# Expert buffers with two experts' rows side by side in 944 slots, and the first expert layer on 64-row tiles

## The chip, the cores and the metric

One NeuronCore of one Trainium2 chip runs the whole program in one launch. The metric is device time in microseconds (us) of that core. The kernel before took 1568.96 us, the median of 3 runs (1568.46 to 1574.54).

## What is computed

Two layers over x with batch B = 8, length L = 750, width D = 64, float32: a dilated convolution, attention and a switch feed-forward (layer 0), then phase attention and a second mixture of experts (layer 1), each added to the running activations `h`. The change is in the layer-0 feed-forward, which sends each of the 6000 tokens to one of 8 experts, with a capacity of C = 938 tokens for each:

```python
C = max(1, math.ceil(1.25 * T / E))                      # T = 6000, E = 8: 938
idx = jnp.argmax(probs, axis=-1)                         # expert of each token
pos = (jnp.cumsum(one_hot, axis=0) * one_hot).sum(-1).astype(jnp.int32) - 1
kept = pos < C
buf = jnp.zeros((E, C, D), dtype=h.dtype).at[idx, pos_safe].set(x, mode='drop')
hmid = jax.nn.relu(jnp.einsum('ecd,edf->ecf', buf, w1) + b1[:, None, :])   # F = 256
ybuf = jnp.einsum('ecf,efd->ecd', hmid, w2) + b2[:, None, :]
y_tok = ybuf[idx, jnp.minimum(pos, C - 1)] * (prb * kept)[:, None]
```

## The kernel before

The instructions of each engine are written out in order, with semaphores between them. Activations `H` and normalized ones `XN` lie in on-chip memory as 125 partitions x 6 tiles for each batch. Two buffers lie in DRAM: `xbuf` (the page calls it expert_in) and `ybuf` (expert_out), each of 8 experts x 1000 rows of 64 floats.

**The start.** GpSimd clears the conv matrix, the identity and a 125 x 512 block `zeros`. SP's queue then issues, in this order: the convolution's small loads, eight fills of `xbuf` with zeros (L972), 18 preparation loads (`prep`, L976: Q, K, VO and small weights), and the later weights (`wd`, L978). TensorE runs nine dependent convolution steps (L517); after step 4's matmuls it waits for all `prep` loads and transposes Q and K (L528), and goes on with step 5. The attention's small copies of row maxima (L988) come behind all of these on SP.

**Routing.** Beside the attention of batch b + 1, and for the last batch behind all attention, VectorE finds each token's expert. GpSimd adds up the one-hot rows of the tiles (kind "choose"), TensorE turns them into positions, GpSimd computes `slot_in` and `slot_out` (kind "slots", ten small operations, each linked to the one before), and issues six scatters of 125 rows into `xbuf` (L1182).

**The expert stage.** After the last attention step GpSimd clears `w1p`; SP waits for that and loads the expert weights: `w1p` holds for each expert a 128-row matrix with its 64 rows in the half that its data use and zeros in the other, `w2e` the second layer. When all 48 scatters have landed, SP loads `xbuf` into `XB` (L1002): expert e in columns 0 to 63, e + 4 in columns 64 to 127, row c x 125 + r of an expert in partition r, chunk c; eight loads. TensorE waits for all eight, transposes 8 chunks for each of four pairs into `XBT` (L737), and waits for the weights. Then it goes on in the order in(0), in(1), out(0), in(2), out(1), back(0), in(3), out(2), back(1), out(3), back(2), back(3). `expert_in` (L748) is 8 matmuls over 128 rows and 469 columns, `expert_out` (L760) 8 matmuls, two in column halves of a bank, `expert_back` (L772) 8 transposes. A float32 matmul is two instructions in the profile. ScalarE and VectorE empty the eight PSUM banks in turn. SP stores a pair as two transfers (L1009) when both its `yb` banks are emptied. GpSimd waits for all eight stores and gathers token rows (L1202), on which the second layer of the network stands.

```python
sp.dma_start(xbuf[e * ROWS:(e + 1) * ROWS].rearrange("(r c) d -> r (c d)", r=R), zeros)          # L972
pe.wait_ge(S["xb_loaded"], 16 * 8)
pool.wait_ge(S["y_stored"], 16 * 8)
```

Of the kernel before, what the change touches and what calls it, by code (L numbers as in the profile page):

```python
# [17 lines left out]
ALU = mybir.AluOpType  # L18
ACT = mybir.ActivationFunctionType
# [11 lines left out]
CAP = -(-(5 * B * L) // (4 * E0))  # L31
CH = CAP // 2
ROWS = 1000
PH, PP, WN = 4, 32, 5
# [16 lines left out]
def build(nc, t, out):  # L51
    with ExitStack() as ctx:
# [115 lines left out]

        w1p, at = view(0, [E0, F0])
        w2e, at = view(at, [E0, 2, D])  # L170
        XB, at = view(at, [4, 8, 128], parts=R)
        XBT, at = view(at, [4, ROWS])
        HM, at = view(at, [2, 2, 2, CAP])
        YT, at = view(at, [4, ROWS])
# [51 lines left out]
        def sem(*names):  # L226
# [12 lines left out]
            "att_h", "rc_ready", "lnb_sum", "lnb_x", "lnb_ssq", "lnb_done", "onehot_sum", "pos_ready", "memory", "big_set", "dma_prep")  # L239
        sem("late_zero", "w_late", "big", "route_ld", "route_ex", "onehot", "slots", "scattered", "xb_loaded",  # L240
            "y_stored", "gathered0", "gathered1", "gathered2", "gathered3",
# [263 lines left out]
        def _(pe):  # L505
# [225 lines left out]

            pe.wait_ge(S["xb_loaded"], 16 * 8)
            for e in range(4):
                for h in range(2):
                    ps, done = take(pe, ("xbt", e, h))
                    for n in range(4):
                        last = pe.transpose(ps[:, n * R:(n + 1) * R], XB[:, e, 4 * h + n, :], ident[0:R, 0:R])  # L737
                    last.then_inc(done, 1)
            pe.wait_ge(S["w_late"], 16 * 3)

            def expert_in(e):
                emptied(pe, ("xbt", e, 0))
                emptied(pe, ("xbt", e, 1))
                for a in range(2):
                    for fh in range(2):
                        for nn in range(2):
                            ps, done = take(pe, ("h1", e, a, fh, nn))
                            pe.matmul(ps[:, 0:CH], w1p[:, e + 4 * a, fh * 128:(fh + 1) * 128],  # L748
                                      XBT[:, e, nn * CH:(nn + 1) * CH], start=True, stop=True).then_inc(done, 1)

# [14 lines left out]
            def expert_back(e):  # L765
                emptied(pe, ("y", e, 0))
                emptied(pe, ("y", e, 1))
                pe.wait_ge(S["big"], 2)
                for h in range(2):
                    ps, done = take(pe, ("yb", e, h))  # L770
                    for n in range(4):
                        last = pe.transpose(ps[0:R, n * 128:(n + 1) * 128],  # L772
                                            YT[:, e, (4 * h + n) * R:(4 * h + n + 1) * R], ident)
                    last.then_inc(done, 1)
# [183 lines left out]
        def _(sp):  # L958
# [12 lines left out]
            for e in range(E0):  # L971
                sp.dma_start(xbuf[e * ROWS:(e + 1) * ROWS].rearrange("(r c) d -> r (c d)", r=R), zeros)\  # L972
                    .then_inc(S["xbuf_zero"], 16)
# [18 lines left out]

            sp.wait_ge(S["late_zero"], 1)
            sp.dma_start(w1p[0:64, 0:4, :], t["L0_ffn_w1"][0:4].rearrange("e d f -> d e f")).then_inc(S["w_late"], 16)
            sp.dma_start(w1p[64:128, 4:8, :], t["L0_ffn_w1"][4:8].rearrange("e d f -> d e f")).then_inc(S["w_late"], 16)
            sp.dma_start(w2e.rearrange("f e h d -> f (e h) d"),
                         t["L0_ffn_w2"].rearrange("e (h f) d -> f (e h) d", h=2)).then_inc(S["w_late"], 16)
            sp.wait_ge(S["scattered"], 16 * NG)
            for e in range(4):
                for a in range(2):  # L1000
                    r0 = (e + 4 * a) * ROWS
                    sp.dma_start(XB[:, e, :, a * D:(a + 1) * D],  # L1002
                                 xbuf[r0:r0 + ROWS].rearrange("(c r) d -> r c d", r=R)).then_inc(S["xb_loaded"], 16)
            for e in range(4):
                emptied(sp, ("yb", e, 0))
                emptied(sp, ("yb", e, 1))
                for a in range(2):
                    r0 = (e + 4 * a) * ROWS
                    sp.dma_start(ybuf[r0:r0 + ROWS].rearrange("(c r) d -> r c d", r=R),  # L1009
                                 XB[:, e, :, a * D:(a + 1) * D]).then_inc(S["y_stored"], 16)  # L1010

            sp.wait_ge(S["late_zero"], 2)
            for a in range(2):
# [16 lines left out]
        def _(pool):  # L1030
# [76 lines left out]
            for job in order:  # L1107
# [44 lines left out]
                elif kind == "choose":  # L1152
                    b = job[1]
                    pool.wait_ge(S["onehot"], b + 1)
                    link(pool.tensor_copy(SO[:, 0, :], SO[:, NJ, :]))
                    for j in range(NJ):
# [4 lines left out]
                elif kind == "slots":  # L1161

                    b = job[1]
                    tiles = slice(NJ * b, NJ * b + NJ)
                    pool.wait_ge(S["pos_ready"], b + 1)
                    link(pool.tensor_scalar(kept, pos, float(CAP), None, ALU.is_le))
                    link(pool.tensor_tensor(pk[:, tiles], prob[:, tiles], kept, ALU.mult))
                    link(pool.tensor_scalar(sl, im, float(ROWS), float(E0 * ROWS), ALU.mult, ALU.add))
                    link(pool.tensor_scalar(tx, kept, -65536.0, 65535.0, ALU.mult, ALU.add))
                    link(pool.tensor_tensor(sx, sl, pos, ALU.add))  # L1170
                    link(pool.tensor_tensor(sx, sx, tx, ALU.add))
                    link(pool.tensor_copy(slot_in[:, tiles], sx))
                    link(pool.tensor_scalar(sy, pos, float(CAP), -1.0, ALU.min, ALU.add))
                    link(pool.tensor_tensor(sy, sy, sl, ALU.add))
                    link(pool.tensor_copy(slot_out[:, tiles], sy))
                    if b == 0:
                        pool.wait_ge(S["xbuf_zero"], 16 * E0)
                elif kind == "scatter":
                    _, b, j = job
                    p, a = b % NP, b // NP  # L1180
                    g = b * NJ + j
                    pool.indirect_dma_start(out=xbuf, out_offset=bass.IndirectOffsetOnAxis(ap=slot_in[:, g:g + 1],  # L1182
                                                                                           axis=0),
                                            in_=XN[:, p, j, a, :], in_offset=None, bounds_check=E0 * ROWS - 1,
                                            oob_is_err=False).then_inc(S["scattered"], 16)
                if job == after[0]:

                    pool.wait_ge(S["st_done"], 3 * NQ)
                    pool.memset(w1p, 0.0).then_inc(S["late_zero"], 1)
                    pool.wait_ge(S["late_zero"], 1)  # L1190


            pool.memset(big[:, 0:1], 1.0e4)
            pool.memset(big[:, 1:2], -1.0e4).then_inc(S["big"], 1)
            pool.memset(YT[:, :, CAP:ROWS], 0.0).then_inc(S["big"], 1)
            pool.wait_ge(S["y_stored"], 16 * 8)

# [85 lines left out]
        def _(act):  # L1283
# [122 lines left out]
            for e in range(4):  # L1406
                copy_out(("xbt", e, 0), XBT[:, e, 0:4 * R])
            for kind, e in ffn_order:
                if kind == "h1":
                    for a in range(2):  # L1410
                        for nn in range(2):
                            name = ("h1", e, a, 0, nn)
                            ps, done = filled(act, name)
                            act.activation(HM[:, e % 2, a, 0, nn * CH:(nn + 1) * CH], ps[:, 0:CH], ACT.Relu,
                                           bias=W["b1"][:, 2 * (e + 4 * a):2 * (e + 4 * a) + 1]).then_inc(done, 1)
                elif kind == "y":
# [128 lines left out]
        def _(dve):  # L1545
# [179 lines left out]
            for e in range(4):  # L1725
                copy_out(("xbt", e, 1), XBT[:, e, 4 * R:8 * R])
            for kind, e in ffn_order:
                if kind == "h1":
                    for a in range(2):
                        for nn in range(2):  # L1730
                            name = ("h1", e, a, 1, nn)
                            ps, done = filled(dve, name)
                            i = 2 * (e + 4 * a) + 1
                            dve.tensor_scalar(HM[:, e % 2, a, 1, nn * CH:(nn + 1) * CH], ps[:, 0:CH],
                                              W["b1"][:, i:i + 1], 0.0, ALU.add, ALU.max).then_inc(done, 1)
                elif kind == "yb":
                    copy_out(("yb", e, 1), XB[:, e, 4:8, :].rearrange("r c d -> r (c d)"))
# [266 lines left out]
```

## Time and profile before

| | us |
|---|---|
| median of 3 runs | 1568.96 |
| profiled execution, its own time | 1570.73 |
| its span, the base of all times below | 1568.7 |
| TensorE matmul busy | 1207.7 (77%) |
| VectorE busy | 875.9 (56%) |
| GpSimd busy | 609.5 (39%) |
| ScalarE busy | 603.9 (39%) |
| hardware DMA queue of SP | 41453 packets, 11.06 MB, 3.4% of 16 engines |

A busy share is an average over stages with different limits, so the table says little about the stretches that the diff touches. "DMA share" in a window is the mean busy share of the core's 16 DMA engines. TensorE's granted clock averages 0.856 of full speed. In the page the start lies in slices 0 and 1 of 40 (39 us each), the expert stage in slices 24 to 26.

### The profile page before, as it was taken

The numbers are of one execution on the slowest core, as the hardware profiler recorded it, in microseconds if no ns is written. First come the engines' busy times: TensorE is split into PE (matmuls) and PEld (weight loads), VectorE is DVE, ScalarE is ACT, GpSimd is POOL, SyncE is SP. The second block draws the span as 40 slices with busy tenths as digits, with TensorE's granted clock in tenths as the row PEclk, the third lists the DMA queues.
The fourth block names the chain that finished last, engine by engine and source line by source line (L and its number), as shares of the span: only waits on it lengthen the run. The fifth ranks groups of instructions, "written<-read, shape, count | busy, mean of one in ns | idle before, by whom it ended". The sixth has DMA issues, their size and how long they took to land.

```text
span 1568.7 us, 25828 instructions
## 1 busy us (share of the span) xinstructions
PE 1207.7 (77%) x9805; PEld 787.0 (50%) x9805; DVE 875.9 (56%) x1807; ACT 603.9 (39%) x961; POOL 609.5 (39%) x1187
## 2 busy tenths in 40 slices
PE   5689999999999999999999922900455868546995
PEld 3345565555556565566655621400335647444664
DVE  3433555554555565555655320305688988743798
ACT  1223545444444444444444400400424335122552
POOL 3100344643544445444454540047744262550000
PEclk9767999999999999999999965955775758666998
DMA  2200000000000000000000012021100000000000
GB/s 73 22 1 1 2 2 2 3 5 2 3 2 2 2 2 2 2 2 2 2 2 2 2 27 53 19 45 16 13 1 1 1 1 1 10 1 0 11 15 15
DMA packets 46182, 14.61 MB, mean 9 GB/s; under 512 B 43386, under 2 KB 44506, under 8 KB 46061
## 3 DMA queue, kind: packets, MB, share of 16 engines
q1 hardware_dynamic: 41453, 11.06, 3.4%
q0 software_dynamic: 4608, 1.91, 1.4%
q8 instruction: 79, 1.29, 0.4%
q14 instruction: 42, 0.34, 0.1%
HBM read 6.67 MB, written 7.17 MB: 9 GB/s over the span
## 4 chain that ended last, share of the span: by engine, by line
PE 60%; DVE 23%; POOL 6%; issue 5%; SPq 3%; DMA 2%; ACT 1%; POOLq 0%; DVEq 0%; ACTq 0%
PE psum L698 19%; PE psum L607 10%; PE psum L679 7%; PE psum L670 7%; PE psum L654 3%; DVE arena L1971 3%; PE psum L592 2%; DVE arena L1970 2%; PE psum L748 2%; DVE arena L1965 1%; SPq L1002 1%; POOL lnst L1088 1%; DVE arena L1651 1%; PE psum L612 1%; SPq L976 1%
## 5 line engine op out<-in xcount | busy, mean ns | idle before, releaser
L1359 ACT ACTIVATE arena<-psum 125x1000 f32<-125x1000 f32 x288 | 289.2, 1004 | 367.9 <-PE psum L679 366.7
L1648 DVE TENSOR_REDUCE arena<-psum 125x1 f32<-125x500 f32 x384 | 243.4, 674 | 254.0 <-PE psum L607 253.8
L607 PE MATMUL psum<-arena 32*125 32x500 f32 (+1 forms) x1536 | 351.9, 525 | 0.5 <-ACT arena L1351 0.5
L698 PE MATMUL psum<-arena,XN 125*64 125x250 f32 x2304 | 311.4, 391 | 0.1
L679 PE MATMUL psum<-arena 32*125 32x250 f32 x2304 | 295.7, 373 | 0.0
L679 PEld LDWEIGHTS psum<-arena 32*125 32x125 f32 x2304 | 215.2, 184 | 10.8 <-issue 0.9
L698 PEld LDWEIGHTS psum<-arena,XN 125*64 125x64 f32 x2304 | 141.4, 137 | 131.9 <-issue 86.8
L1651 DVE TENSOR_REDUCE arena<-psum 125x2 f32<-125x500 f32 x192 | 121.5, 674 | 74.6 <-PE psum L607 71.3
L607 PEld LDWEIGHTS psum<-arena 32*125 32x125 f32 x1536 | 149.0, 186 | 8.6 <-ACT arena L1351 4.1
L670 PE MATMUL psum<-arena,onesb 3*125 3x500 bf16 x576 | 123.2, 425 | 4.5 <-DMA arena<-arena 4.5
L1117 POOL TENSOR_SCALAR arena<-arena 125x4 bf16<-125x4 f32 x96 | 22.1, 231 | 237.8 <-DVE arena L1656 236.6
L1202 POOL DMA_INDIRECT XN<-expert_out,slot_out x48 | 63.2, 1317 | 107.1 <-DMA expert_out<-arena 93.2
L567 PE MATMUL psum<-ident,XN 125*128 125x125 f32 x84 | 18.0, 378 | 91.5 <-POOL XN L1089 73.8
L1131 POOL TENSOR_TENSOR arena<-arena 125x512 f32<-125x512 f32 x46 | 48.2, 1048 | 90.5 <-DVE arena L1702 90.4
L670 PEld LDWEIGHTS psum<-arena,onesb 3*125 3x125 bf16 x576 | 38.1, 129 | 85.2 <-issue 76.1
L654 PE MATMUL psum<-vox,arena 64*125 64x65 f32 x768 | 52.3, 273 | 32.2 <-issue 15.5
L1133 POOL TENSOR_TENSOR arena<-arena 125x256 f32<-125x256 f32 x138 | 69.5, 504 | 10.8
L1536 ACT ACTIVATE arena<-psum,wall 128x375 f32<-128x375 f32 x96 | 55.0, 574 | 44.0 <-PE psum L925 37.9
L654 PEld LDWEIGHTS psum<-vox,arena 64*125 64x125 f32 x768 | 47.0, 185 | 49.5 <-issue 49.5
L1182 POOL DMA_INDIRECT expert_in<-XN,slot_in x48 | 59.8, 1247 | 27.6 <-issue 13.8
L834 PE MATMUL psum<-ident,arena 125*128 125x125 f32 x48 | 17.2, 367 | 68.9 <-DVE arena L1859 68.7
L1088 POOL TENSOR_TENSOR lnst<-lnst,mhalf 125x12 f32<-125x12 f32 x14 | 32.2, 2298 | 96.8 <-DVE lnst L1627 96.8
(328 smaller groups left out, 2036.8 us busy)
## 6 DMA issues: line engine op xcount, KB each, us to landing
arena<-arena SPq DMA_DIRECT2D x192, 1.5 KB
expert_in<-XN SPq DMA_DIRECT2D x8, 250.0 KB
arena<-expert_in SPq DMA_DIRECT2D x8, 250.0 KB
expert_out<-arena SPq DMA_DIRECT2D x8, 250.0 KB
out<-H SPq DMA_DIRECT2D x8, 187.5 KB
expert_in<-XN,slot_in POOLq DMA_INDIRECT x48
XN<-expert_out,slot_out POOLq DMA_INDIRECT x48, 3.9
arena<-in_L_ffn_w SPq DMA_DIRECT2D x2, 256.0 KB, 4.1
```

Of the source, the lines that this page charges most:

```text
L607: last = pe.matmul(ps[0:R, at_:at_ + hi - lo], QH[row:row + 32, b, g, j * R:(j + 1) * R], KH[row:row + 32, b, g, lo:hi], start=True, stop= ...
L654: last = pe.matmul(ps[0:R, hp * (D + 1):(hp + 1) * (D + 1)], CT[r, b % 2, hp, j * R:(j + 1) * R], vox[r, hp, h * (D + 1):(h + 1) * (D + 1) ...
L670: pe.matmul(st_bank[x % 2][h2][0:R, 0:2 * THIRD].rearrange("r (i c) -> r i c", i=2), onesb[row:row + 3, 0:R], NS_[row:row + 3, m % 3, :].u ...
L679: last = pe.matmul(st_bank[x % 2][h2][0:R, i * THIRD:(i + 1) * THIRD], KH[row:row + 32, b, g, c * R:(c + 1) * R], QH[row:row + 32, b, g, t ...
L698: last = pe.matmul(ctx_bank[64 * h2:64 * h2 + 64, 0:THIRD], XN[:, p, c, a, :], PR[:, x % 4, h2, i * THIRD:(i + 1) * THIRD], start=(c == 0) ...
L1133: link(pool.tensor_tensor(OT[:, 0:w], OT[:, 0:w], OT[:, w:2 * w], ALU.add))
L1182: pool.indirect_dma_start(out=xbuf, out_offset=bass.IndirectOffsetOnAxis(ap=slot_in[:, g:g + 1], axis=0), in_=XN[:, p, j, a, :], in_offset ...
L1202: pool.indirect_dma_start(out=XN[:, p, j, a, :], out_offset=None, in_=ybuf, in_offset=bass.IndirectOffsetOnAxis(ap=slot_out[:, g:g + 1], a ...
L1359: act.activation(PR[:, x % 4], psum[0:R, 3 + 2 * (x % 2):5 + 2 * (x % 2), 0:2 * THIRD], ACT.Exp)\
L1536: act.activation(dst, ps[:, 0:HALF], ACT.Relu, bias=b_).then_inc(done, 1)
L1648: dve.reduce_max(MX[:, q % 2, 0, 2 * h2 + tile:2 * h2 + tile + 1], ps[0:R, 0:2 * THIRD], AX)\
L1651: dve.reduce_max(MX[:, q % 2, 1, 2 * h2:2 * h2 + 2], ps[0:R, 0:2 * THIRD].rearrange("r (n c) -> r n c", n=2), AX).then_inc(done, 1)
```

## The change

- An expert has 944 slots, 118 partitions x 8 (`RW` = 118, `ROWS` = 944, `CH` = 472 columns in a half, before 469).
- Experts are stored pairwise: pair e holds e and e + 4, with slot s of both side by side, 512 B. Slot s lies in partition s / 8, chunk s mod 8, so one partition's piece of a pair is 4 KB, contiguous on both sides. There are four loads and four stores, and TensorE waits for each pair's load by itself.
- In `slots`, row index = 2 x ROWS x e + 2 x position - 2, and for experts 4 to 7 one more and 8 x ROWS less. Three operations that need only the expert stand in "choose" now; "slots" has eight.
- `w1p` is half as large, experts e and e + 4 in its two 64-row halves, without zeros; its clearing is gone, and SP waits for the last attention scores instead. `expert_in` multiplies 64-row tiles, (0, 0) and (64, 0) in turn, into different banks. ScalarE empties those of e, VectorE those of e + 4.
- `YT` has no rest to be cleared; TensorE's wait for it is gone.
- The zero fills of `xbuf` use 118 partitions.

```diff
-CH = CAP // 2
-ROWS = 1000
+RW = -(-CAP // 8)
+ROWS = 8 * RW
+CH = ROWS // 2
...
-            pe.wait_ge(S["xb_loaded"], 16 * 8)
             for e in range(4):
+                pe.wait_ge(S[f"xb_loaded{e}"], 16)
                 for h in range(2):
                     ps, done = take(pe, ("xbt", e, h))
                     for n in range(4):
-                        last = pe.transpose(ps[:, n * R:(n + 1) * R], XB[:, e, 4 * h + n, :], ident[0:R, 0:R])
+                        last = pe.transpose(ps[:, n * RW:(n + 1) * RW], XB[:, e, 4 * h + n, :], ident[0:RW, 0:RW])
...
-                for a in range(2):
-                    for fh in range(2):
-                        for nn in range(2):
+                for fh in range(2):
+                    for nn in range(2):
+                        for a in range(2):
+                            r = slice(64 * a, 64 * a + 64)
                             ps, done = take(pe, ("h1", e, a, fh, nn))
-                            pe.matmul(ps[:, 0:CH], w1p[:, e + 4 * a, fh * 128:(fh + 1) * 128],
-                                      XBT[:, e, nn * CH:(nn + 1) * CH], start=True, stop=True).then_inc(done, 1)
+                            pe.matmul(ps[:, 0:CH], w1p[r, e, fh * 128:(fh + 1) * 128],
+                                      XBT[r, e, nn * CH:(nn + 1) * CH], start=True, stop=True,
+                                      tile_position=(64 * a, 0)).then_inc(done, 1)
...
             for e in range(E0):
-                sp.dma_start(xbuf[e * ROWS:(e + 1) * ROWS].rearrange("(r c) d -> r (c d)", r=R), zeros)\
+                sp.dma_start(xbuf[e * ROWS:(e + 1) * ROWS].rearrange("(r c) d -> r (c d)", r=RW), zeros[0:RW, :])\
                     .then_inc(S["xbuf_zero"], 16)
...
-            sp.wait_ge(S["late_zero"], 1)
+            sp.wait_ge(S["st_done"], 3 * NQ)
...
             for e in range(4):
-                for a in range(2):
-                    r0 = (e + 4 * a) * ROWS
-                    sp.dma_start(XB[:, e, :, a * D:(a + 1) * D],
-                                 xbuf[r0:r0 + ROWS].rearrange("(c r) d -> r c d", r=R)).then_inc(S["xb_loaded"], 16)
+                sp.dma_start(XB[:, e].rearrange("r c x -> r (c x)"),
+                             xbuf[2 * e * ROWS:2 * (e + 1) * ROWS].rearrange("(r c) d -> r (c d)", r=RW))\
+                    .then_inc(S[f"xb_loaded{e}"], 16)
             for e in range(4):
                 emptied(sp, ("yb", e, 0))
                 emptied(sp, ("yb", e, 1))
-                for a in range(2):
-                    r0 = (e + 4 * a) * ROWS
-                    sp.dma_start(ybuf[r0:r0 + ROWS].rearrange("(c r) d -> r c d", r=R),
-                                 XB[:, e, :, a * D:(a + 1) * D]).then_inc(S["y_stored"], 16)
+                sp.dma_start(ybuf[2 * e * ROWS:2 * (e + 1) * ROWS].rearrange("(r c) d -> r (c d)", r=RW),
+                             XB[:, e].rearrange("r c x -> r (c x)")).then_inc(S["y_stored"], 16)
...
                     pool.wait_ge(S["onehot"], b + 1)
+                    link(pool.tensor_scalar(sx, im, -4.0, float(1 - E0 * ROWS), ALU.is_ge, ALU.mult))
+                    link(pool.tensor_scalar(sl, im, float(2 * ROWS), float(2 * E0 * ROWS - 2), ALU.mult, ALU.add))
+                    link(pool.tensor_tensor(sl, sl, sx, ALU.add))
...
-                    pool.wait_ge(S["st_done"], 3 * NQ)
-                    pool.memset(w1p, 0.0).then_inc(S["late_zero"], 1)
...
-            pool.memset(YT[:, :, CAP:ROWS], 0.0).then_inc(S["big"], 1)
-            pool.wait_ge(S["y_stored"], 16 * 8)
+            pool.wait_ge(S["y_stored"], 16 * 4)
```

## Rows read from the trace of the kernel before

**Rows 1.** Page, part 4: shares of the chain that ended last, by engine.

```profile
PE 60%; DVE 23%; POOL 6%; issue 5%; SPq 3%; DMA 2%; ACT 1%; POOLq 0%; DVEq 0%; ACTq 0%
```

**Rows 2.** Chain of waits, 0 to 120 us: start us, us, what.

```profile
9.68 0.27 SPq L972
...
15.84 2.51 SPq L972
...
18.39 1.46 SPq L976
...
25.58 0.95 SPq L976
...
32.57 3.10 DMA arena<-in_L_attn_pos_phases
...
35.71 1.97 PE psum L528 x8
```

**Rows 3.** Timeline of TensorE, 18 to 60 us: start, us, instruction, [idle before].

```profile
35.71 1.97 PE L528 MATMUL psum<-ident,arena 128*128 128x128 f32 x8 [0.28 <-DMA arena<-in_L_attn_pos_phases]
```

**Rows 4.** Chain of waits, 830 to 1060 us: start us, us, what.

```profile
884.67 0.84 PE psum L679 x8
...
943.67 0.30 SPq L1002
...
962.80 8.96 DMA arena<-expert_in
971.80 5.71 PE psum L737 x32
977.51 12.61 PE psum L748 x32
990.11 3.30 PE psum L760 x16
...
1003.21 1.07 PE psum L772 x8
...
1027.32 7.68 DMA expert_out<-arena
```

**Rows 5.** Windows, zero fills: busy us of PE, PEld, DVE, ACT, POOL; PEclk, DMA share, GB/s.

```profile
10.00:15.00 5.00, 0.34 (x1) 0.34 (x2) 4.87 (x12) 0.00 (x0) 4.33 (x7) 1.00 0.29 91
15.00:20.00 5.00, 3.85 (x12) 2.75 (x12) 1.87 (x5) 1.75 (x2) 0.00 (x0) 1.00 0.33 127
```

**Rows 6.** Windows, the expert loads (first row) and stores (second).

```profile
952.00:955.00 3.00, 0.00 (x0) 0.00 (x0) 0.00 (x0) 0.00 (x0) 0.00 (x0) 0.50 0.41 78
...
1024.00:1028.00 4.00, 0.00 (x0) 0.00 (x0) 0.00 (x0) 0.00 (x0) 0.00 (x0) 0.50 0.40 90
```

**Rows 7.** Windows, the late expert weights.

```profile
907.50:909.00 1.50, 0.70 (x14) 0.60 (x12) 0.86 (x4) 0.00 (x0) 0.00 (x0) 1.00 0.77 229
909.00:911.00 2.00, 0.95 (x16) 0.81 (x16) 1.90 (x5) 0.00 (x0) 0.00 (x0) 1.00 1.25 198
```

**Rows 8.** Windows, TensorE's clock behind the expert loads.

```profile
975.50:976.00 0.50, 0.50 (x4) 0.50 (x3) 0.50 (x1) 0.00 (x0) 0.00 (x0) 0.50 0.00 0
...
976.50:977.00 0.50, 0.50 (x7) 0.50 (x6) 0.31 (x1) 0.35 (x1) 0.00 (x0) 1.00 0.00 0
```

**Rows 9.** Groups of instructions by form, 880 to 1060 us: first-layer evictions.

```profile
L1734 DVE TENSOR_SCALAR arena<-psum,wall 128x469 f32<-128x469 f32 x16 | 11.3, 706 | 17.5 <-PE psum L748 16.8
...
L1414 ACT ACTIVATE arena<-psum,wall 128x469 f32<-128x469 f32 x16 | 10.4, 653 | 11.2 <-PE psum L748 10.1
```

**Rows 10.** Timeline of SP's queue, 972 to 1062 us.

```profile
1005.10 25.10 SPq L1009 DMA_DIRECT2D expert_out<-arena  x8
```

**Rows 11.** Timeline of GpSimd, 900 to 935 us.

```profile
904.31 1.80 POOL L1189 MEMSET arena<- 128x2048 f32 x1 [2.93 <-PE psum L679]
913.75 0.25 POOL L1141 TENSOR_SCALAR arena<-arena 125x6 f32<-125x6 f32 x1 [7.63 <-DVE arena L1693]
...
926.01 1.61 POOL L1157 TENSOR_TENSOR arena<-arena 125x8 f32<-125x8 f32 x6
```

More of the change, by code:

```diff
@@ L166, in build @@
         r1, at = view(at, [9, NJ], parts=R)
-        w1p, at = view(0, [E0, F0])
+        w1p, at = view(0, [4, F0])
         w2e, at = view(at, [E0, 2, D])
-        XB, at = view(at, [4, 8, 128], parts=R)
+        XB, at = view(at, [4, 8, 128], parts=RW)
         XBT, at = view(at, [4, ROWS])
-        HM, at = view(at, [2, 2, 2, CAP])
+        HM, at = view(at, [2, 2, 2, ROWS])
         YT, at = view(at, [4, ROWS])
@@ L239, in build @@
             "att_h", "rc_ready", "lnb_sum", "lnb_x", "lnb_ssq", "lnb_done", "onehot_sum", "pos_ready", "memory", "big_set", "dma_prep")
-        sem("late_zero", "w_late", "big", "route_ld", "route_ex", "onehot", "slots", "scattered", "xb_loaded",
+        sem("late_zero", "w_late", "big", "route_ld", "route_ex", "onehot", "slots", "scattered", "xb_loaded0", "xb_loaded1", "xb_loaded2", "xb_loaded3",
             "y_stored", "gathered0", "gathered1", "gathered2", "gathered3",
@@ L767, in expert_back @@
                 emptied(pe, ("y", e, 1))
-                pe.wait_ge(S["big"], 2)
                 for h in range(2):
@@ L771, in expert_back @@
                     for n in range(4):
-                        last = pe.transpose(ps[0:R, n * 128:(n + 1) * 128],
-                                            YT[:, e, (4 * h + n) * R:(4 * h + n + 1) * R], ident)
+                        last = pe.transpose(ps[0:RW, n * 128:(n + 1) * 128],
+                                            YT[:, e, (4 * h + n) * RW:(4 * h + n + 1) * RW], ident)
                     last.then_inc(done, 1)
@@ L990, in _ @@
                             .then_inc((S["shift_dma0"], S["shift_dma1"])[q % 2], 16)
-            sp.wait_ge(S["late_zero"], 1)
-            sp.dma_start(w1p[0:64, 0:4, :], t["L0_ffn_w1"][0:4].rearrange("e d f -> d e f")).then_inc(S["w_late"], 16)
-            sp.dma_start(w1p[64:128, 4:8, :], t["L0_ffn_w1"][4:8].rearrange("e d f -> d e f")).then_inc(S["w_late"], 16)
+            sp.wait_ge(S["st_done"], 3 * NQ)
+            sp.dma_start(w1p[0:64], t["L0_ffn_w1"][0:4].rearrange("e d f -> d e f")).then_inc(S["w_late"], 16)
+            sp.dma_start(w1p[64:128], t["L0_ffn_w1"][4:8].rearrange("e d f -> d e f")).then_inc(S["w_late"], 16)
             sp.dma_start(w2e.rearrange("f e h d -> f (e h) d"),
@@ L1006, in _ @@
                 emptied(sp, ("yb", e, 1))
-                for a in range(2):
-                    r0 = (e + 4 * a) * ROWS
-                    sp.dma_start(ybuf[r0:r0 + ROWS].rearrange("(c r) d -> r c d", r=R),
-                                 XB[:, e, :, a * D:(a + 1) * D]).then_inc(S["y_stored"], 16)
-            sp.wait_ge(S["late_zero"], 2)
+                sp.dma_start(ybuf[2 * e * ROWS:2 * (e + 1) * ROWS].rearrange("(r c) d -> r (c d)", r=RW),
+                             XB[:, e].rearrange("r c x -> r (c x)")).then_inc(S["y_stored"], 16)
+            sp.wait_ge(S["late_zero"], 1)
             for a in range(2):
@@ L1165, in _ @@
                     pool.wait_ge(S["pos_ready"], b + 1)
+                    link(pool.tensor_scalar(tx, pos, float(CAP), 65536.0, ALU.is_gt, ALU.mult))
+                    link(pool.tensor_scalar(sy, pos, float(CAP), 2.0, ALU.min, ALU.mult))
+                    link(pool.tensor_tensor(sy, sy, sl, ALU.add))
+                    link(pool.tensor_tensor(sx, sy, tx, ALU.add))
+                    link(pool.tensor_copy(slot_in[:, tiles], sx))
+                    link(pool.tensor_copy(slot_out[:, tiles], sy))
                     link(pool.tensor_scalar(kept, pos, float(CAP), None, ALU.is_le))
                     link(pool.tensor_tensor(pk[:, tiles], prob[:, tiles], kept, ALU.mult))
[L1168 to L1175, printed above, removed]
                     if b == 0:
@@ L1185, in _ @@
                                             oob_is_err=False).then_inc(S["scattered"], 16)
-                if job == after[0]:
-                    pool.wait_ge(S["st_done"], 3 * NQ)
-                    pool.memset(w1p, 0.0).then_inc(S["late_zero"], 1)
-                    pool.wait_ge(S["late_zero"], 1)
-            pool.memset(big[:, 0:1], 1.0e4)
+            pool.memset(big[:, 0:1], 1.0e4).then_inc(S["big"], 1)
             pool.memset(big[:, 1:2], -1.0e4).then_inc(S["big"], 1)
-            pool.memset(YT[:, :, CAP:ROWS], 0.0).then_inc(S["big"], 1)
-            pool.wait_ge(S["y_stored"], 16 * 8)
+            pool.wait_ge(S["y_stored"], 16 * 4)
             def gather(p, js=range(NJ)):
@@ L1406, in _ @@
             for e in range(4):
-                copy_out(("xbt", e, 0), XBT[:, e, 0:4 * R])
+                copy_out(("xbt", e, 0), XBT[:, e, 0:CH])
             for kind, e in ffn_order:
                 if kind == "h1":
-                    for a in range(2):
+                    for fh in range(2):
                         for nn in range(2):
[L1412 to L1415, printed above, removed]
+                            ps, done = filled(act, ("h1", e, 0, fh, nn))
+                            act.activation(HM[:, e % 2, 0, fh, nn * CH:(nn + 1) * CH], ps[:, 0:CH], ACT.Relu,
+                                           bias=W["b1"][:, 2 * e + fh:2 * e + fh + 1]).then_inc(done, 1)
                 elif kind == "y":
@@ L1725, in _ @@
             for e in range(4):
-                copy_out(("xbt", e, 1), XBT[:, e, 4 * R:8 * R])
+                copy_out(("xbt", e, 1), XBT[:, e, CH:ROWS])
             for kind, e in ffn_order:
                 if kind == "h1":
-                    for a in range(2):
+                    for fh in range(2):
                         for nn in range(2):
[L1731 to L1734, printed above, removed]
+                            ps, done = filled(dve, ("h1", e, 1, fh, nn))
+                            i = 2 * (e + 4) + fh
+                            dve.tensor_scalar(HM[:, e % 2, 1, fh, nn * CH:(nn + 1) * CH], ps[:, 0:CH],
                                               W["b1"][:, i:i + 1], 0.0, ALU.add, ALU.max).then_inc(done, 1)
```

## The prediction

> **What bounds the kernel now.** I began with the chain of waits [rows 1]: TensorE holds 60% of it, and data movement stands on it in two forms, as issue time of SP (SPq, 3%) and as transfers (DMA, 2%). The page names SP's lines 976 and 1002, both near the lines of the diff, so I followed the chain through the two stretches that touch the expert buffers.
>
> The first is the start [rows 2]. SP issues eight zero fills of the expert buffer (L972), 9.68 to 18.35 us, then 18 preparation loads (L976). The last of those lands at 32.57 + 3.10 = 35.67 us, and TensorE starts L528 at 35.71. How tight this is stands in TensorE's own row [rows 3]: it had been idle 0.28 us for that load. So whatever delays the preparation loads is paid at once by everything behind.
>
> The second is the expert stage, 943.67 to 1035 us [rows 4]: loads 28.1 us (first issue to 971.80), expert matmuls until the last eviction near 1020, and a store tail that lands at 1035.0. TensorE has no other work here and gathers can only start after the last store.
>
> **How many DMA engines work.** This decides the case. The transfer rate over the zero fills, with SP's queue backed up behind them, was 127 GB/s at a DMA share of 0.33 [rows 5]. The expert loads ran at 78 GB/s and share 0.41, the stores at 90 and 0.40, also backed up [rows 6]. All three have 125 rows outermost. The late weights have 64 and 128 rows and reach share 1.25 and over 200 GB/s [rows 7]. A share of 1.25 for sixteen engines means that one engine counts up to 1.25 times when its packets overlap; 0.41 / 1.25 x 16 = 5.2 engines, 0.33 at an overlap near 1 is 5.3. So a 125-row transfer runs on five engines, and five is the largest number up to 16 that divides 125. My reading of these rows is that rows are dealt out in equal shares. Then 118 = 2 x 59 leaves two engines. The change makes pieces larger but cuts the engines from five to two, and the zero fills, with the same 2 KB pieces, only lose.
> The Trainium skill says so outright (DMA: Bandwidth & Descriptors, section "Why a DMA increments its semaphore by 16 and not by 1"): a transfer uses the largest count up to 16 that divides the outermost size of both sides. By that rule 125 gives 5, with which the shares above agree, and 118 gives 2, which no row here can show; the sum below goes by it and by my reading of the rows alike.
>
> The rate of one engine: zero fills, 127 / 5 = 25.4 GB/s with 2 KB pieces; expert loads 78 / 5 = 15.6 with 256 B pieces. For 4 KB pieces I take the nearer row, 25.4, so 50.8 GB/s for a transfer on two engines. Ends for the range: 20 (half way to the 256 B rate, if reads of 4 KB don't reach the fills' rate) and 28.
>
> **Start: +22 us.** Fills after: 8 x 118 x 2 KB = 1.933 MB at 50.8 = 38.1 us, against 2.048 MB at 127 = 16.1. How SP is held: by 18.35 us, when the eighth fill is issued, 5 x 91 + 3.35 x 127 = 880 KB had moved [rows 5], so 1168 KB or 570 pieces stood ahead, 114 on each of five engines. Data flowed as if it had begun at 18.35 - 880/127 = 11.4 us. After: 8 x 59 = 472 pieces per engine, 80.6 ns each (2048 / 25.4). The eighth issue ends when 472 - 114 = 358 are gone: 11.4 + 28.9 = 40.3 us. The six loads that follow (Q, K, four of VO: 128 or 64 rows, some 16 pieces on each engine) were throttled too, 18.39 to 25.53 us; after, 96 slots per engine at 80.6 ns = 7.7 us, to 48.0. The last twelve are not held now (25.58 to 32.57, 7.0 us [rows 2]) and won't be: 55.0, landing 3.1 later at 58.1 against 35.67: **+22.4**. Low end: SP is not held at all, and the loads' shares on the two busy engines merely queue behind fills that end at 11.4 + 38.1 = 49.5, plus 3: +17. High end at 20 GB/s an engine: fills 48.3 us, +33. Nothing covers it, since convolution step 5 and everything behind stand after L528. SP's later weight loads and its first shift copy move back by the same amount, so they gain no new overlap or collision. The fills' own consumer, the first scatter near 305 us, stays covered.
>
> **Expert loads: the last one +11.7 us.** Fixed part now: 28.1 - 2.048 MB / 78 (26.3) = 1.8 us. After: 4 x 483 KB = 1.933 MB at 50.8 = 38.1, with 1.8 = 39.9. One load lands every 9.5 us, and pairs 0 to 2 are transposed meanwhile, but `expert_in(0)` stands behind the transposes of pair 3 in TensorE's order. The last transposes start at 943.67 + 39.9 = 983.5, now 971.80.
>
> **Expert matmuls: -12.3 us from the last load to the first store.** Behind the last load only 8 transposes remain (now 32 in 5.71 us). The clock was 0.50 until 976.0 and 1.00 from 976.5 [rows 8], about 4.3 us after TensorE became busy; so 8 transposes at 0.21 = 1.6 us, then first-layer work at half speed for 2.7 us. First layer: now 32 instructions in 12.61 us, 0.394 each [rows 4]. Do pairs of row tiles overlap? Score matmuls, 32-row tiles in turn, took 0.84 us for 8 of 250 columns, 0.105 each [rows 4]; at L748's 0.84 ns a column one alone would be 0.210. So two do run side by side, as the column pairs of L760 do (0.206). I take 0.199 for 472 columns; the other end is 0.397 (no overlap), a rival below. Pairs 0 and 1, 32 instructions: 7 in the slow 2.7 us, 25 x 0.199 = 5.0. Then second layer 3.3, first layer 3.2, second 3.3, back-transposes 1.1 [rows 4]: 1.6 + 2.7 + 5.0 + 3.3 + 3.2 + 3.3 + 1.1 = 20.2, so 1003.7, where now it is 1004.3 (32.5 behind the last load). Eviction keeps up: two banks (one for ScalarE, one for VectorE) every 0.79 us against 0.65 and 0.71 us an eviction [rows 9].
>
> **Stores: +9 us at the stage's end.** First issue now 1005.10 [rows 10], after 1004.5 (0.8 behind those transposes, as now). The remaining pairs are ready at intervals of at most 7.6 us, less than one store of 9.5, so the stores run back to back: 1004.5 + 39.9 = 1044.4, now 1035.0: **+9.4** for the stage. The faster first layer is thus swallowed: it only feeds a queue that is full.
>
> **GpSimd: +0.3.** Three operations move into `choose` and the slot computation goes from ten to eight, each some 0.27 us (1.61 / 6) [rows 11]. For the last batch both stand on the chain: 3 - 2 = 1 operation. For the seven batches before, they lie beside attention. The memset of w1p (1.8 us at 904.31, then idle until 913.75) was hidden, so removing it gives nothing; the three weight loads start some 1.8 us sooner, long before use. The YT memset and its waits lay beside the loads: 0. If any of this cover went, it would be 2 us.
>
> Sum: 22.4 + 9.4 + 0.3 = +32.1 us on a profiled execution of 1570.73 (span 1568.7). The median of the runs is 1568.96; I put the difference on that: **1601 us**.
>
> **Rivals.**
> A: the engine count stays five. For it: nothing in the trace shows a 118-row transfer. Against: five fits only a divisor of 125. Start 0; a load 483 KB / 127 = 3.8 us, the last at 943.67 + 1.8 + 15.2 = 960.7; from there 33.3 us to the last back-transposes (20.2 + 3.2 + 3.3 + 1.1 + 3.3 + 1.1 + 1.1), 0.7 eviction, 1.8 + 3.8 for the last store: 1000.3, -35 us: 1534.
> B: all sixteen work. Then at the 229 GB/s of [rows 7] a load is 2.1 us; last load 953.9, stage end 953.9 + 34.0 + 3.9 = 991.8: -43, 1526. Against: 125-row shares a third of the 128-row ones.
> C: two engines, but the start hides it (preparation loads are served beside the fills): only +10, 1579. Against: the loads and the fills share the queue, and SP's issues were already stretched by it.
> D: two engines and row tiles don't overlap: the first store waits for pairs 0 to 2; they take 48 x 0.199 = 9.5 us more, and the whole store queue moves with it: 1610.
>
> **Chances.** Forecast 0.67 (own range 1590 to 1614), D 0.08, C 0.10, A 0.07, B 0.06, something else small 0.02. Low 1577 takes in C; high 1616 takes in D and most of the slow-engine end. What a measurement can tell from no change is 0.5%, 8 us. Faster 0.13, within 0.02, slower 0.85.
>
> **What would show it.** Right: DMA share near 0.13 to 0.16 with some 51 GB/s through the fills, the expert loads and the stores; the eighth L972 issue ending near 40 us; L528 starting near 58 us with some 22 us of idle time before it, ended by the last preparation load; expert loads landing 9.4 us apart; first-layer instructions at 0.2 us; the stage from the last scatter to the first gather 100.8 us where it is 91.4. Wrong: the fills at 127 GB/s again, or L528 where it was. If both stretches shrink, the engine count is not what the rows made me think, and the sign is wrong.

## The result and the profile after

The changed kernel took 1607.58 us (median of 4 runs, 1598.38 to 1609.4), a ratio to the kernel before of 1.0223, 95% interval 1.0176 to 1.0269: 2.2% slower, clear of no change, though not clear of 2%. (The ratios go by means, of six executions here, and not by medians.) In a second session (e5 below) it gave 1609.0 us and 1.022 (1.0174 to 1.0267). The kernel before itself stands elsewhere in other sessions: its median was 1568.48 us beside e1 to e4 and 1577.06 us beside e5 to e8, so an experiment's time is to be read by its ratio. One further execution of the kernel before took 5077.07 us and is in no median or ratio. The profiled execution below is the quickest of the changed kernel, 1598.38 us with a span of 1596.3.

The start, in the chain of waits of the changed kernel (start us, us, what), against [rows 2]:

```profile
9.65 0.25 SPq L974
...
32.16 4.37 SPq L974
...
36.58 4.98 SPq L978
...
54.42 3.04 DMA arena<-in_L_attn_pos_phases
...
57.51 1.97 PE psum L529 x8
```

The eighth fill is issued by 36.53 us (18.35 before), the last preparation load lands at 57.46 (35.67). TensorE's row, against [rows 3], shows what it costs; the number in brackets is its idle time ahead of the row:

```profile
57.51 1.97 PE L529 MATMUL psum<-ident,arena 128*128 128x128 f32 x8 [22.13 <-DMA arena<-in_L_attn_pos_phases]
```

0.28 us of waiting became 22.13. The windows of the zero fills (busy times, then granted clock, DMA share, GB/s), against [rows 5], and of the expert loads and stores, against [rows 6]:

```profile
15.00:20.00 5.00, 3.85 (x12) 2.71 (x12) 1.90 (x5) 1.75 (x2) 0.00 (x0) 1.00 0.13 52
...
35.00:40.00 5.00, 0.38 (x3) 0.25 (x1) 0.82 (x2) 0.47 (x1) 0.00 (x0) 1.00 0.13 51
```

```profile
975.00:980.00 5.00, 0.68 (x4) 0.31 (x2) 0.65 (x1) 0.49 (x1) 0.00 (x0) 0.50 0.13 52
...
1050.00:1060.00 10.00, 0.00 (x0) 0.00 (x0) 0.00 (x0) 0.00 (x0) 0.00 (x0) 0.50 0.13 52
```

All four stand at share 0.13 and 51 to 52 GB/s, where they were 0.33, 0.41 and 0.40. It makes no difference whether pieces are 2 KB or 4 KB or which way they go: on two engines that is 26 GB/s for each. A share times 16 is the mean number of pieces in flight, 0.13 x 16 = 2.1 here.

The expert stage in the chain of waits, against [rows 4]:

```profile
961.92 0.27 SPq L1002
...
969.71 32.03 DMA arena<-expert_in
1001.78 1.84 PE psum L738 x8
1003.62 8.29 PE psum L750 x32
1011.91 3.32 PE psum L763 x16
1015.23 3.37 PE psum L750 x16
...
1021.91 1.02 PE psum L774 x8
...
1036.65 26.19 DMA expert_out<-arena
```

From the first load (961.92) to the first gather's release (1036.65 + 26.19 = 1062.84) it takes 100.9 us, where it took 91.3. TensorE's timeline shows the loads coming in, 9.4 us apart, each followed by eight transposes and idle time:

```profile
973.85 1.83 PE L738 MATMUL psum<-ident,arena 118*128 118x118 f32 x8 [26.26 <-DMA arena<-expert_in]
983.22 1.83 PE L738 MATMUL psum<-ident,arena 118*128 118x118 f32 x8 [7.54 <-DMA arena<-expert_in]
```

Stretches of all profiled executions, in us. "Start wait" is TensorE's idle time for preparation loads; "middle" runs from the Q and K transposes to the first expert load, "stage" from there to the landing of the last store, "rest" to the end. The clocks in brackets are the mean granted clock of TensorE in a window 60 to 100 us behind those transposes, and 330 to 440 us behind the stage.

| kernel | rows of a fill | fills GB/s | start wait | middle (clock) | stage | rest (clock) | ratio to before |
|---|---|---|---|---|---|---|---|
| before | 125 | 127 | 0.28 | 908.0 (0.59) | 91.3 | 533.7 (0.72) | 1 |
| changed | 118 | 52 | 22.13 | 904.4 (0.67) | 100.9 | 533.5 (0.72) | 1.0223 |
| e5, changed again | 118 | 51 | 22.23 | 909.1 (0.59) | 101.1 | 539.4 (0.66) | 1.0220 |
| e1, fills split | 112 + 6 | 288 | 0 | 906.2 (0.59) | 100.9 | 539.6 (0.66) | 1.0096 |
| e2, all split | 112 + 6 | 284 | 0 | 915.1 (0.50) | 47.5 | 537.9 (0.66) | 0.9739 |
| e3, 120 rows | 120 | 312 | 0 | 915.0 (0.50) | 49.3 | 534.0 (0.72) | 0.9747 |
| e4, 125 rows | 125 | 127 | 0.35 | 908.8 (0.59) | 65.9 | 537.9 (0.66) | 0.9887 |
| e8, 119 rows | 119 | 175 | 0 | 908.2 (0.59) | 57.1 | 539.5 (0.64) | one run |
| e6, tiles undone | 118 | 51 | 22.11 | 909.0 (0.59) | 111.8 | 539.5 (0.64) | 1.0279 |
| e7, tiles only | 125 | 127 | 0.36 | 903.3 (0.68) | 79.0 | 541.5 (0.65) | 0.9937 |

The fill rate is that of 12 to 15 us for e1 to e3, whose fills are over soon after, of 15 to 17.5 us for e8, and of 15 to 20 us for the others. e8 has one execution; the other ratios have intervals in their sections.

### The profile page after: what moved, and what is told of

Read it like the earlier page. It is cut to its first block, busy times and chain, and to the rows that moved or that the text cites. A ratio compares the mean times of both kernels' runs of the same rounds, so it can differ in the third digit from the quotient of the medians.

```text
span 1596.3 us, 25824 instructions
## 1 busy us (share of the span) xinstructions
PE 1194.4 (75%) x9805; PEld 778.9 (49%) x9805; DVE 876.5 (55%) x1807; ACT 603.0 (38%) x961; POOL 608.5 (38%) x1193
## 4 chain that ended last, share of the span: by engine, by line
PE 58%; DVE 22%; POOL 6%; issue 5%; DMA 5%; SPq 3%; ACT 1%; POOLq 0%; DVEq 0%; ACTq 0%
PE psum L699 18%; PE psum L608 10%; PE psum L680 7%; PE psum L671 6%; PE psum L655 3%; DVE arena L1962 2%; DMA arena<-expert_in 2%; PE psum L593 2%; DVE arena L1961 2%; SPq L974 2%; DMA expert_out<-arena 2%; DVE arena L1956 1%; POOL lnst L1087 1%; SPq L978 1%; DVE arena L1643 1%
## 5 line engine op out<-in xcount | busy, mean ns | idle before, releaser
L655 PEld LDWEIGHTS psum<-vox,arena 64*125 64x125 f32 x768 | 47.0, 185 | 49.5 <-issue 49.5
L1182 POOL DMA_INDIRECT expert_in<-XN,slot_in x48 | 59.7, 1244 | 27.7 <-issue 13.8
```

Source lines behind the costliest of these rows:

```text
L655: last = pe.matmul(ps[0:R, hp * (D + 1):(hp + 1) * (D + 1)], CT[r, b % 2, hp, j * R:(j + 1) * R], vox[r, hp, h * (D + 1):(h + 1) * (D + 1) ...
```

## The experiments

**e1: only the engine count of the fills.** The changed kernel; each fill goes out in two transfers whose row counts have larger divisors.

```diff
-                sp.dma_start(xbuf[...].rearrange("(r c) d -> r (c d)", r=RW), zeros[0:RW, :])\
-                    .then_inc(S["xbuf_zero"], 16)
+                for r in (slice(0, 112), slice(112, RW)):
+                    sp.dma_start(fill[r], zeros[r, :]).then_inc(S["xbuf_zero"], 16)
```

> The changed kernel with one edit: each zero fill of 118 rows is issued as two transfers, of 112 rows and of 6 rows. Same bytes, same 2 KB pieces; 112 is divisible by 16, 6 runs on six engines. Theory (engines follow a divisor of the row count): the fills no longer hold SP, the preparation loads land near 31 us and no longer end TensorE's wait; L529-type transposes start near 35.5 us where the changed kernel has 57.5; the time is 22 us below the changed kernel, that is some +10 us against before; the expert stage stays at 101 us. Rival (118-row transfers are slow for another reason, such as the 3.8 KB row pitch or the sheer number of bytes in one queue): splitting rows changes nothing and it stays +32 us, or gets worse through eight more issues.

Measured: 1583.75 us, ratio 1.0096 (1.0060 to 1.0132). SP's queue, TensorE's timeline and a window of this kernel:

```profile
9.65 6.20 SPq L976 DMA_DIRECT2D expert_in<-XN  x16
```

```profile
35.20 1.95 PE L529 MATMUL psum<-ident,arena 128*128 128x128 f32 x8
```

```profile
10.00:15.00 5.00, 0.37 (x1) 0.38 (x2) 4.84 (x12) 0.00 (x0) 4.30 (x7) 1.00 0.80 255
```

All sixteen fills are issued in 6.2 us instead of 26.9 for eight, and the transposes start at 35.20 without a wait for a load. DMA share is 0.80 in the window shown, which takes in the first 0.4 us without a piece; from 12 to 15 us it is 0.89, at 288 GB/s. Same bytes and pieces on the same queue: the rival that blames bytes or pitch is out (a row of `xbuf` follows the one before at 2 KB, not at 3.8). The start gives back 22.4 us in the profiles (57.61 to 35.20); the ratios of e5 and e1 differ by 0.0124, 19 us. Against the kernel before the medians differ by 15.3 us, where 10 was expected; the interval (9 to 21 us) holds both. In the profile the last stretch is 5.9 us longer than before, at a lower clock, to which I come below.

**e2: the expert transfers too.** Loads and stores of a pair are split in the same way at row 112.

> As the first, and the four loads and four stores of expert pairs are split into 112 and 6 rows too (4 KB pieces, the same bytes). Theory: a pair's load takes 1.4 to 2.1 us instead of 9.4 (229 to 350 GB/s); last scatter to first gather 46 to 50 us where the changed kernel has 101 and before has 91.4; the time is 41 to 45 us below before, near 1526 us. Rival (two engines were not the limit, the 4 KB pieces are): the stage stays at 101 us and the time is that of the first kernel.

Measured: 1529.52 us, ratio 0.9739 (0.9700 to 0.9779). Chain of waits and a window in the loads:

```profile
952.14 6.96 DMA arena<-expert_in
...
993.88 3.90 DMA expert_out<-arena
```

```profile
952.00:954.00 2.00, 0.00 (x0) 0.00 (x0) 0.00 (x0) 0.00 (x0) 0.00 (x0) 0.50 1.04 285
```

The last load lands 8.8 us behind the first issue instead of 39.8, the stage takes 47.5 us. The 4 KB pieces run at up to 285 GB/s, so they never were the limit; the 350 GB/s at the upper end of what was expected appear in no run. The layout is good; only its row count is not.

**e3: 120 rows.**

```diff
-RW = -(-CAP // 8)
+RW = 120
```

> The changed kernel with RW = 120 in place of 118: 960 slots to an expert, 1.7% more bytes and columns. 120 = 15 x 8. Theory: fifteen engines in fills, loads and stores; fills no longer felt (TensorE's wait for preparation under 1 us), stage 46 to 50 us, time near 1526 us. Rival (more rows, more bytes, nothing else): 1 to 2 us slower than the changed kernel.

Measured: 1531.26 us, ratio 0.9747 (0.9703 to 0.9791). Loads and stores in windows:

```profile
952.00:954.00 2.00, 0.00 (x0) 0.00 (x0) 0.00 (x0) 0.00 (x0) 0.00 (x0) 0.50 0.98 262
...
996.00:998.00 2.00, 0.00 (x0) 0.00 (x0) 0.00 (x0) 0.00 (x0) 0.00 (x0) 1.00 0.92 274
```

262 and 274 GB/s. Two rows more, 1.7% more bytes, and the kernel is 4.8 percentage points quicker than the changed one and 2.5% quicker than the kernel before. With e2 it is the version that beats both; the two can't be told apart by their times.

**e4: 125 rows in the new layout,** that is the engine count of the kernel before (`RW = 125`), my rival A.

> The changed kernel with RW = 125: 1000 slots, 5.9% more bytes and columns than with 118, the same piece sizes. 125 = 5 x 25. Theory: five engines, 127 GB/s; start as before the change (TensorE's wait 0.3 us); loads of 512 KB 4.0 us each; stage 58 to 61 us; time 31 to 34 us below before, near 1537 us. DMA share 0.33 in fills and loads. Rival (slowness by bytes): slower than the changed kernel by about 6% of its transfer time, 6 us.

Measured: 1550.3 us, ratio 0.9887 (0.9840 to 0.9933). Window of the fills, TensorE's wait, and the chain:

```profile
15.00:20.00 5.00, 3.85 (x12) 2.72 (x12) 1.90 (x5) 1.75 (x2) 0.00 (x0) 1.00 0.33 127
```

```profile
35.74 1.97 PE L529 MATMUL psum<-ident,arena 128*128 128x128 f32 x8 [0.35 <-DMA arena<-in_L_attn_pos_phases]
```

```profile
945.63 17.11 DMA arena<-expert_in
...
998.20 12.21 DMA expert_out<-arena
```

Fills at share 0.33 and 127 GB/s with a wait of 0.35 us are the start of the kernel before again, and the last load lands at 962.74, 18.2 us behind the first issue, as worked out (1.8 + 4 x 4.03 = 17.9). The direction and the start came as expected; the size did not: 18 us below before instead of 31 to 34. The stage is 65.9 us, not 58 to 61. The chain shows where: 12.2 us from the last store's issue, where I had reckoned one store (5.8); rival A of the prediction counts one store in the same way. Pairs 2 and 3 are ready close together, so two stores stand in the queue. A further 4.2 us lie in the last stretch (537.9 against 533.7), which the kernel does not change; what is left of the gap is within the interval.

**e8: 119 rows, between 118 and 120** (`RW = 119`, one execution).

> The changed kernel with RW = 119 = 7 x 17: one row more than 118, one less than 120. Theory: seven engines, fills at 7 x 25.4 = 178 GB/s and share 0.44 to 0.50, between the 51 GB/s of 118 and the 268 of 120; TensorE's wait for preparation gone; a pair's load 487 KB / 178 = 2.7 us, all four 12.8 us with the fixed 1.8; stage 52 to 56 us. Rival (only multiples of 5 or 8 are fast): fills at 51 GB/s or less, wait 22 us or more.

Measured: 1541.98 us in its one run. Window and chain:

```profile
15.00:20.00 5.00, 3.85 (x12) 2.71 (x12) 1.91 (x5) 1.75 (x2) 0.00 (x0) 1.00 0.49 183
```

```profile
944.45 12.49 DMA arena<-expert_in
...
991.64 8.82 DMA expert_out<-arena
```

183 GB/s at share 0.49, and no wait. The window also holds loads that SP issued from 17.54 us on; the fills alone, 15 to 17.5 us, show 175 GB/s at share 0.46. Rates of the fills over the row count: 118 gives 51, 119 175, 120 312, 125 127. No smooth function of rows or bytes does that; the largest divisor up to 16 does, with 2, 7, 15 and 5 engines and 25.5, 25.0, 20.8 and 25.4 GB/s for each. Fifteen no longer reach the rate of one alone.

The packet records in the kept traces show the count without a rate. Of the 2 KB pieces of the fills exactly two were in flight for 90% of 15 to 20 us in the changed kernel, five for 80% of 13 to 18 us in the kernel before, seven for 69% of 12 to 17.5 us here, and fifteen for 45% of 12 to 14.5 us with 120 rows. The rest of the time is mostly one more, with fifteen also one less. The median piece took 84 ns in each of the four. With the 4 KB pieces of the expert loads it was two for 96% of the window shown above for the changed kernel, five for 89% in e4, seven for 84% here and fifteen for 59% in e3.

The last row of the chain is again two stores, so the stage is 1 us above its expected end.

**e5 and e6: what the tiles are worth in the changed kernel.** e5 is the changed kernel unedited; e6 has the first layer back on padded 128-row weights, with their clearing on GpSimd.

> The changed kernel once more, unedited, as the base for the next kernel on the same chip. Expected: TensorE's wait for preparation 22.1 us, stage 101.0 us, as in its first profile; time 1.5 to 2.5% above before. The stretch between (from the Q and K transposes to the first expert load) took 904 to 915 us in six profiles although no edit touches its work; if that is the clock that TensorE is granted in its first part, this run's stretch goes with the clock of its windows from 60 to 120 us behind those transposes, not with the kernel.

> The changed kernel with its first expert layer back on zero-padded 128-row weights (w1p of eight matrices, cleared on GpSimd, SP waiting for that), all else as changed: two-engine transfers, 4 KB pieces. Theory: first-layer instructions 0.394 us instead of 0.2; the first store waits for the first layer of pairs 0 to 2, so it and the whole store queue come 9.0 to 9.5 us later: stage 110 us, time 9 us above the changed kernel. Rival (the sentence of the prediction that the faster first layer is swallowed by the full store queue): stage 101 us, no difference.

```diff
-                            pe.matmul(ps[:, 0:CH], w1p[r, e, fh * 128:(fh + 1) * 128],
-                                      XBT[r, e, nn * CH:(nn + 1) * CH], ..., tile_position=(64 * a, 0))
+                            pe.matmul(ps[:, 0:CH], w1p[:, e + 4 * a, fh * 128:(fh + 1) * 128],
+                                      XBT[:, e, nn * CH:(nn + 1) * CH], ...)
```

Measured: e5 1609.0 us, e6 1618.87 us, 9.9 above; ratios 1.0220 and 1.0279 (1.0234 to 1.0324). Chain of e6, then SP's stores in e6 and e5:

```profile
1008.17 14.54 PE psum L749 x32
...
1053.59 24.76 DMA expert_out<-arena
```

```profile
1037.72 18.00 SPq L1006 DMA_DIRECT2D expert_out<-arena  x4
```

```profile
1028.64 16.43 SPq L1008 DMA_DIRECT2D expert_out<-arena  x4
```

The first 32 first-layer instructions take 14.54 us (8.29 in the changed kernel). The first store goes out 71.2 us behind the first load instead of 61.9, and the stage is 111.8 against 101.1. The executions do not overlap either (1607.37 to 1613.54 us against 1617.87 to 1621.73). So the tiles are worth 10 us inside the changed kernel; they are not swallowed.

**e7: the tiles alone in the kernel before.** Same edit of `expert_in`, weights and evictions; buffers, slots and transfers as before.

> The kernel before with the 64-row tiles alone: w1p of four double matrices, first layer on tiles in turn, evictions split as changed; buffers, slots, eight loads and stores as before, and w1p's region still cleared. Theory: first store 9.3 us sooner, last pair ready 12.5 us sooner; stage 91.4 - 12.6 = 79 us (stores 5.7 us a pair, the last three back to back), time 12 us below before, 0.8%. Rival (tiles don't overlap at 128 columns and 64 rows, or evictions can't follow): first-layer instructions stay at 0.39 us and the time is that of before.

Measured: 1564.03 us, ratio 0.9937 (0.9910 to 0.9964). Chain:

```profile
972.86 6.50 PE psum L749 x32
...
1010.50 7.54 DMA expert_out<-arena
```

32 instructions in 6.50 us where [rows 4] has 12.61. The rows of these matmuls (least, median and greatest ns of one), first in e7, then in the kernel before:

```profile
L749 PE MATMUL psum<-arena x44: 551/553/657, 972.8 to 984.7; 64*128 64x469 f32 x44
```

```profile
L748 PE MATMUL psum<-arena x20: 554/556/562, 977.3 to 984.8; 128*128 128x469 f32 x20
```

One takes as long as before, but in e7 two start within 6 ns of each other and the next two 0.39 us later, where the kernel before starts one every 0.39 us. So pairs of 64-row tiles with 128 columns run side by side, and the evictions follow. The stage is 79.0 us, as expected. In the profile the stage gives 12.3 us and the middle 4.7, while the rest takes back 7.8; the ratio's 0.63% is 10 us, and its interval (6 to 14 us) holds the 12.

## Why the prediction was right

**Engines by a divisor of the rows: shown.** The forecast stood on one inference, five engines at 125 rows, therefore two at 118. The changed kernel's share of 0.13 and 51 GB/s fit it. e1 shows it by splitting the rows of the same bytes, and e3, e4 and e8 by one constant each, which moves the row count and at most 6% of the bytes; the pieces in flight are two, five, seven and fifteen as forecast. The rule of the Trainium skill that the prediction cited (DMA: Bandwidth & Descriptors, "Why a DMA increments its semaphore by 16 and not by 1") agrees at 118, 119, 120 and 125 rows.

**Start, +22.4: right,** 21.8 measured (35.71 to 57.51). The queue model was right in size and wrong in detail, so part of this closeness is luck. It let 114 pieces wait on each engine when the eighth issue ends; the packet records show 115 on each of five before, but 162 on each of two after. So the eighth issue ended at 36.5 us, not 40.3. The six loads behind it then took 10.7 us to issue (Q alone 5.0) and not 7.7, which made up for most of it. The low end and rival C (the loads served beside the fills) are out. The prediction named the first scatter as the only consumer of the fills; VectorE also waits for them before it first overwrites `XN`, at 83.6 us, long after the last piece landed at 49.5, so it cost nothing.

**Loads, +11.7: right.** First issue to last transposes 39.9 us, forecast 39.9.

**Matmuls: right.** From the last load to the end of pair 0's back-transposes: 21.2 us, forecast 20.2. Eight transposes took 1.84 (forecast 1.6), the first 32 instructions, partly at half clock, 8.29 (7.7), the next 16 3.37 (3.2). The clock stayed at 0.50 for 5.3 us behind the last load, where the sum has 4.3. The first store went out 61.8 us behind the first load, forecast 60.8.

**Stores, +9.4: the size was right, a sentence on it wrong.** The stage grew by 9.6 us. But "the faster first layer is thus swallowed" does not hold: e6 shows 10 us for it. The step that failed is the one that took a full queue for cover. The first store waits for the first layer of pairs 0 to 2, and all stores stand behind the first; only pair 3's share is swallowed. The prediction's own rival D had priced this at 9.5 us; D as a forecast fell, since the tiles do overlap.

**GpSimd, +0.3:** from `choose`'s first operation to the first scatter 8.22 us where it was 7.86. Right.

**What the sum left out.** The three steps measured 21.8 + 9.6 + 0.4 = 31.8 us, forecast 32.1. The median moved further, 38.6 us, to 1607.6 where 1601 was forecast. That the excess of 6 us is real is not shown: the interval of the ratio is 28 to 42 us and holds 32.1, and in e5's session, with 13 executions of the kernel before, the medians are 31.9 us apart (1609.0 and 1577.06). The two profiled executions of the result are only 27.7 us apart, because the middle of the changed one is 3.6 us shorter.

The middle and the rest contain the same work in every kernel here but for GpSimd's 0.3 us, and yet vary by 12 and 8 us in the table. They go with TensorE's granted clock in part of them. Windows 60 to 100 us behind the Q and K transposes in e3, e5 and the first profile of the changed kernel (granted clock is the third number from the end):

```profile
95.20:135.20 40.00, 38.08 (x147) 20.77 (x147) 13.49 (x24) 7.97 (x12) 3.20 (x15) 0.50 0.00 1
```

```profile
117.50:157.50 40.00, 38.65 (x167) 21.26 (x161) 15.27 (x28) 9.83 (x15) 3.20 (x15) 0.59 0.01 1
```

```profile
117.50:157.50 40.00, 37.93 (x182) 21.05 (x180) 16.22 (x31) 9.80 (x15) 3.97 (x19) 0.67 0.01 1
```

At 0.50 the middle took 915 us, at 0.59 906 to 909, at 0.67 and 0.68 904 and 903; TensorE was busy nearly all the time in each. The expectation of e5 had named this part beforehand, and e5 to e8 followed it. That the clock is the cause is not shown, for the whole middle does not tell the kernels apart by it: its mean clock is 0.94 to 0.95 in all ten, and over the first 120 us it is 0.70 both in e1 (906 us) and in e3 (915). For the rest, the changed kernel's first profile and e5:

```profile
1392.90:1502.90 110.00, 70.96 (x365) 54.76 (x366) 52.16 (x109) 35.41 (x71) 26.66 (x17) 0.72 0.01 1
```

```profile
1397.80:1507.80 110.00, 72.34 (x342) 57.69 (x342) 47.43 (x100) 32.57 (x67) 26.66 (x17) 0.66 0.00 1
```

At 0.72 the rest took 533.5 to 534.0 us (three profiles), at 0.64 to 0.66 537.9 to 541.5 (seven). TensorE was busy for 317.9 to 318.7 us of it in the three and for 319.8 to 326.2 in the seven. The same kernel shows both (changed and e5). Why the clock takes one course or the other stays open.

## What to carry to other kernels

Before a transfer's outermost size is chosen, look at its divisors: 118 rows put sixteen times larger pieces on two engines, and 120 rows would have won 2.5%. The DMA share of a window at a full queue, times 16, says about how many engines carry it. Look also at every other transfer that uses the same constant: two thirds of this loss came from a zero fill that only followed the constant, because SP's queue held the loads behind it. And a full queue hides only the work behind its first entry: whatever the first entry waits for still counts in full.

## What the runs showed of the hardware

- One engine moved 25 to 26 GB/s. With 2 KB pieces two, five and seven engines gave 51, 127 and 175 GB/s together, with 4 KB pieces 52, 131 and 175 (expert loads of the changed kernel, e4 and e8). Fifteen or sixteen gave 262 to 312 GB/s, 17 to 21 each (e1, e2, e3).
- SP held its issues by what waited on the engines: eight fills took 26.9 us to issue on two engines, 8.7 on five, 7.85 on seven, 5.1 on fifteen. When the eighth was through, 115 pieces were left on each of five engines, 162 on each of two.
- Two float32 matmuls on 64-row tiles ran side by side: 32 instructions of 469 columns in 6.50 us instead of 12.61 (e7).
- TensorE's granted clock took different courses in the same stretch of the same kernel. In the changed kernel and e5 it was 0.67 and 0.59 in one window and 0.72 and 0.66 in another, and the stretches around them were 4.7 and 5.9 us longer at the lower one. Together that is more than the 0.5% (8 us) that I had taken as what can be told.
